# Turning the gathered expert tokens by DMA transposes from SyncE instead of by TensorE

## The chip, the core and the metric

The kernel runs on one core of a Trainium2 chip. A core has a matrix engine (TensorE, PE in the rows; its weight loads are PEld), a vector engine (VectorE, DVE), a scalar engine (ScalarE, ACT), GpSimd (POOL) and SyncE (SP), each with its own instruction stream, and sixteen DMA engines that all issuing engines share. The streams are joined only by semaphores. The metric is the device time of one execution in microseconds. Differences of about 0.2% are what a measurement of this kernel can resolve.

## The reference

Four layers run one after the other on 1250 nodes of 1024 features: a message-passing layer with four hops, a feed-forward layer with low-rank additions, a two-layer neighbour mean network, and last a layer of eight experts. Only the last one is touched:

```python
capacity = max(1, int(Sz * CAP_FACTOR / E) + 1)          # 313 of 1250 tokens
scores = softmax(einsum('bsd,ed->bse', x, router_w))
gate_vals, sel_idx = top_k(swapaxes(scores, 1, 2), capacity)
tokens = x[b_idx, sel_idx]
h = gelu(einsum('becd,edh->bech', tokens, w1) + b1)      # 1024 -> 512
y = einsum('bech,ehd->becd', h, w2) + b2                 # 512 -> 1024
out = zeros_like(x).at[b_idx, sel_idx].add(y * gate_vals)
```

Each expert takes the 313 tokens that score highest for it, so which rows it reads is known only at run time.

## The kernel before, in words

Everything up to the router is the same in both kernels. The experts run from about 1274 us to the end. An expert is e = 2i + j, and j is also its buffer: i counts pairs, j is 0 or 1. `over_experts` (line 197) lays out for every engine a `first`, then a hardware loop over two pairs, then experts 4 to 6 written out, and `last` for expert 7. `after(i, j)` is the next expert.

The normalised tokens lie in DRAM (`h_d`), each row as two float16 parts, high and low, of 1024 elements each. The 313 tokens of an expert fill three lists (`SLOTS`) of 128, 128 and 64 rows. For one expert the engines do this:

- PE makes the lists of token numbers (`lists`, L1476, for the first two experts L1468), DVE turns them into indices (`idx`, L2481), and POOL gathers the rows by three indirect DMAs into `gx` (L857), tokens on the partitions.
- The first product needs the features on the partitions. PE therefore turns `gx` in `turn` (L1484 to L1497): 3 lists x 2 parts x 8 blocks = 48 transposes against an identity into PSUM, and ACT (L1790, high parts) and DVE (L2497, low parts) copy each of the six PSUM banks to `tkT`. `tkT` has two buffers, by j. The turn of expert e+1 stands on PE between `ffn1` and `ffn2` of expert e.
- `ffn1` (L1508): 4 groups h of 24 matmuls of 314 columns, `tkT` times `w1b`. ACT applies the gelu to each group (L1798, to `hb`) and makes its high part (L1802, to `hT`), DVE its low part (L2504, semaphore `s_elo`).
- `ffn2` waits for all four low parts, then runs L1528 (4 x 12 matmuls of 512 columns, with `lists(i + 1, j)` for expert e+2 in its middle) and L1534 (the 64-row list). DVE adds the bias (L2528, L2522), ACT multiplies by the gate (L1809), POOL scatters with addition to DRAM (L865).
- The weights come in float32, 2 MB for each of w1 and w2, by SP's DMA to `w_st` (L1054, one slot for each of the two). ACT makes the high parts (`high`, L1783: to `wb` for w1, to `wa` for w2), DVE the low parts (`low`, L2490). A slot is free for the next load when DVE's low part is made (`s_wlo`).
- SP's stream for expert n is short: `weights(n, 0)`, a wait for the outputs of expert n-2 (`s_y`), the bias rows (L1059, L1061, to a piece of `adj`), `weights(n, 1)`. The very first w1 uses a buffer of its own, so in `sp_first` SP loads w2 of expert 0 and biases and at once goes on to `weights` of expert 1.

`filler` on PE (L1289) multiplies constants and has no result; it stands where PE would be idle.

Of the kernel before, what the change touches and what calls it, by code (L numbers as in the profile page):

```python
# [24 lines left out]
NODES, D = 1250, 1024  # L25
# [192 lines left out]
def build(nc, a):  # L218

    with ExitStack() as ctx:  # L220
# [289 lines left out]
        s_etr, s_eev, s_f1, s_f2, s_gelu, s_ehi, s_elo = (sem("s_" + n) for n in ("etr", "eev", "f1", "f2", "gelu", "ehi", "elo"))  # L510
# [20 lines left out]
        s_gn, s_xg, s_xgl = sem("s_gn"), sem2("s_xg"), sem2("s_xgl")  # L531
        s_tick, s_wsh = sem("s_tick"), sem("s_wsh")
# [88 lines left out]
        def _(g):  # L621
# [229 lines left out]
            def gather(i, j):  # L851
                e = 2 * i + j
                g.wait_ge(s_idx, e + 1)
                g.wait_ge(s_etr, 3 * e + 3)
# [28 lines left out]
        def _(sp):  # L883
# [179 lines left out]

            def sp_first():
                weights(0, 0, 1), biases(0, 0)

            def sp_body(i, j, more):
                n = after(i, j)
                weights(*n, 0)
                sp.wait_ge(s_y, 5 * (2 * i + j) + 2)  # L1070
                biases(*n)
                weights(*n, 1)
# [7 lines left out]
        def _(pe):  # L1080
# [380 lines left out]
            def lists(i, j):  # L1461
# [11 lines left out]
                pe.wait_ge(s_eev, 6 * e + 2)  # L1473
# [7 lines left out]
            def turn(i, j):  # L1481

                e = 2 * i + j
                pe.wait_ge(s_eev, 6 * e + 2)  # L1484
                if isinstance(e, int) and e == 0:
                    pe.wait_ge(s_idx, 2)
                for c in range(3):
                    pe.wait_ge(s_gx[j][c], 16 * (i + 1))
                    if c:
                        pe.wait_ge(s_gelu, 4 * e + 2 * c)  # L1490
                    if c == 2:
                        pe.sem_inc(s_tick, 1)
                    for part in range(2):
                        for k in range(KT):
                            n = SLOTS[c][1]
                            ins = pe.transpose(bank16(2 * c + part)[:, k * P:k * P + n],  # L1496
                                               gx[0:n, j, c, part * D + k * P:part * D + (k + 1) * P], ident16[0:n, 0:n])  # L1497
                    ins.then_inc(s_etr, 1)

            def ffn1(i, j):  # L1500
                e = 2 * i + j
                pe.wait_ge(s_wlo, 2 * e + 1)
                pe.wait_ge(s_eev, 6 * e + 8)
# [35 lines left out]
            def body(i, j, more):  # L1539
                ffn1(i, j), turn(*after(i, j))  # L1540
                ffn2(i, j, (lambda: lists(i + 1, j)) if more else none)

            def first():
# [6 lines left out]
                turn(0, 0)  # L1550
# [5 lines left out]
        def _(s):  # L1556
# [228 lines left out]
            def turn(i, j):  # L1785
                e = 2 * i + j
                for c in range(3):
                    s.wait_ge(s_etr, 3 * e + c + 7)
                    at, n = SLOTS[c]
                    s.activation(tkT[:, j, 0, :, at:at + n],  # L1790
                                 bank16(2 * c).rearrange("p (k n) -> p k n", n=P)[:, :, 0:n], ACT.Copy).then_inc(s_eev, 1)

# [18 lines left out]
            def body(i, j, more):  # L1811
                n = after(i, j)
                high(*n, 0), hidden(i, j), turn(*n), high(*n, 1), gates(i, j)
# [4 lines left out]
            s.sem_inc(s_gelu, 4), s.sem_inc(s_yg, 6), s.sem_inc(s_f1, 8), s.sem_inc(s_f2, 10), s.sem_inc(s_etr, 6)  # L1818
            over_experts(lambda a_, b_, _: s.Fori(a_, b_), lambda: (high(0, 0, 1), turn(0, 0)), body,
# [3 lines left out]
        def _(v):  # L1823
# [668 lines left out]
            def turn(i, j):  # L2492
                e = 2 * i + j
                for c in range(3):
                    v.wait_ge(s_etr, 3 * e + c + 7)
                    at, n = SLOTS[c]
                    v.tensor_copy(tkT[:, j, 1, :, at:at + n],  # L2497
                                  bank16(2 * c + 1).rearrange("p (k n) -> p k n", n=P)[:, :, 0:n]).then_inc(s_eev, 1)

# [31 lines left out]
            def body(i, j, more):  # L2531
                n = after(i, j)
                low(*n, 0), hidden(i, j), turn(*n), keep(i, j)
# [54 lines left out]
```

## Time and profile before

| | us |
|---|---|
| median of three runs | 1536.62 (1533.77 to 1537.14) |
| the profiled execution | 1533.59 |
| its span, first to last instruction | 1532.0 |
| of it, experts from the first turn (1286.39) to the end | 246 |
| TensorE busy | 1463.6 (96%) |
| mean granted TensorE clock | 0.99 |

The profile records one execution. "Idle before" a group is the time its engine did nothing ahead of it, and the arrow names what ended that time. TensorE is busy in nearly all of the span, so a time is read first from its stream, and then from the gaps in it.

### The profile page before, as it was taken

The numbers are of one execution on the slowest core, as the hardware profiler recorded it, in microseconds if no ns is written. First come the engines' busy times: TensorE is split into PE (matmuls) and PEld (weight loads), VectorE is DVE, ScalarE is ACT, GpSimd is POOL, SyncE is SP. The second block draws the span as 40 slices with busy tenths as digits, with TensorE's granted clock in tenths as the row PEclk, the third lists the DMA queues.
The fourth block names the chain that finished last, engine by engine and source line by source line (L and its number), as shares of the span: only waits on it lengthen the run. The fifth ranks groups of instructions, "written<-read, shape, count | busy, mean of one in ns | idle before, by whom it ended". The sixth has DMA issues, their size and how long they took to land.

```text
span 1532.0 us, 30009 instructions
## 1 busy us (share of the span) xinstructions
PE 1463.6 (96%) x9131; PEld 770.0 (50%) x9131; DVE 910.6 (59%) x2039; ACT 588.8 (38%) x803; POOL 384.1 (25%) x399
## 2 busy tenths in 40 slices
PE   6799999999999999999999999999999988999996
PEld 5344454545445545444554454445544545656653
DVE  7888879686978887542342222223336577567542
ACT  4677757373524554221111221001112123655552
POOL 5444320202201110000676000810012211243232
PEclk9999999999999999999999999999999998999998
DMA  6000010000244333221422112531033355888963
GB/s 262 22 22 16 14 42 14 24 3 27 74 151 143 123 132 132 108 82 42 140 80 79 45 41 71 186 113 42 0 107 128 123 197 163 253 235 261 286 170 57
DMA packets 57414, 161.37 MB, mean 105 GB/s; under 512 B 6908, under 2 KB 8395, under 8 KB 57336
## 3 DMA queue, kind: packets, MB, share of 16 engines
q1 hardware_dynamic: 45176, 118.42, 21.4%
q0 software_dynamic: 12160, 41.95, 10.6%
q8 instruction: 44, 0.72, 0.2%
q14 instruction: 34, 0.28, 0.1%
HBM read 118.40 MB, written 41.94 MB: 105 GB/s over the span
## 4 chain that ended last, share of the span: by engine, by line
PE 70%; DVE 14%; issue 7%; ACT 3%; POOL 2%; DVEq 1%; DMA 1%; ACTq 0%; SPq 0%; POOLq 0%
PE ps L1297 27%; PE ps L1369 11%; PE ps L1508 7%; PE ps L1528 5%; PE ps L1188 3%; PE ps L1190 3%; PE ps L1189 3%; PE ps L1116 2%; PE ps L595 2%; DVE bstat L550 1%; PE ps L1534 1%; PE ps L1496 1%; ACT th L1608 1%; DVE hm L1985 1%; PE ps L1217 1%
## 5 line engine op out<-in xcount | busy, mean ns | idle before, releaser
L1297 PE MATMUL ps<-wa,tb 128*128 128x512 f16 x960 | 210.1, 379 | 4.3 <-issue 4.1
L1369 PE MATMUL ps<-adj,nm 128*128 128x384 f16 (+2 forms) x960 | 169.6, 340 | 1.6 <-DVEq L2312 1.6
L1188 PE MATMUL ps<-gp,hop 128*128 (+1 forms) x400 | 151.6, 379 | 0.8 <-DVE gn L2061 0.8
L1189 PE MATMUL ps<-gp,hop 128*128 (+1 forms) x400 | 151.6, 379 | 0.0
L1190 PE MATMUL ps<-gp,hop 128*128 (+1 forms) x400 | 151.6, 379 | 0.0
L1297 PEld LDWEIGHTS ps<-wa,tb 128*128 (+1 forms) x960 | 92.8, 98 | 114.5 <-issue 5.4
L1369 PEld LDWEIGHTS ps<-adj,nm 128*128 x960 | 93.9, 98 | 77.2 <-issue 2.1
L1728 ACT ACTIVATE tb<-cx 128x384 f32 (+1 forms) x48 | 26.8, 559 | 259.1 <-DVE cx L2302 259.1
L1297 PE MATMUL ps<-wa,hop 128*128 128x512 f16 x480 | 105.3, 379 | 2.4 <-DVEq L2240 2.4
L1297 PE MATMUL ps<-wb,hop 128*128 128x512 f16 x480 | 105.1, 379 | 0.0
L1297 PE MATMUL ps<-wb,tb 128*128 128x512 f16 x480 | 103.9, 379 | 0.7 <-DVEq L2326 0.7
L1508 PE MATMUL ps<-tkT,wb 128*128 128x314 f16 x768 | 103.8, 297 | 0.8 <-ACT tkT L1790 0.8
L1508 PEld LDWEIGHTS ps<-tkT,wb 128*128 128x128 f16 x768 | 74.5, 98 | 30.6 <-issue 3.8
L2302 DVE TENSOR_TENSOR cx<-ps,dinv_row 128x384 f32<-128x384 f32 (+1 forms) x48 | 28.9, 602 | 99.2 <-PE ps L1369 99.2
L1528 PE MATMUL ps<-wa,hT 128*128 128x512 f16 x384 | 85.2, 379 | 1.7 <-issue 1.7
L686 POOL DMA_DIRECT2D stage<-in_wn x16 | 9.2, 576 | 279.3 <-PE ps L1297 270.4
L1297 PEld LDWEIGHTS ps<-wb,tb 128*128 (+1 forms) x480 | 46.8, 98 | 57.1 <-issue 0.9
L1990 DVE TENSOR_TENSOR hop<-hm,hop 128x640 f32 (+1 forms) x80 | 68.6, 893 | 11.3 <-ACT hop L1613 11.1
L1297 PEld LDWEIGHTS ps<-wa,hop 128*128 128x128 f16 x480 | 46.2, 98 | 57.6 <-DVEq L2240 2.9
L1297 PEld LDWEIGHTS ps<-wb,hop 128*128 128x128 f16 x480 | 46.4, 98 | 55.3 <-issue 0.4
L692 POOL TENSOR_SCALAR stage<-stage 128x1024 f32<-128x1024 f32 x32 | 34.3, 1073 | 155.0 <-DVE bcur L1927 127.6
L1613 ACT ACTIVATE hop<-hm 128x640 f32 (+1 forms) x80 | 58.9, 736 | 33.6 <-DVE hm L1985 33.5
(403 smaller groups left out, 2459.0 us busy)
## 6 DMA issues: line engine op xcount, KB each, us to landing
w_st<-in_ew SPq DMA_DIRECT2D x16, 2048.0 KB, 11.1
self_d<-cr SPq DMA_DIRECT2D x20, 512.0 KB, 2.9
cr<-self_d SPq DMA_DIRECT2D x20, 512.0 KB, 4.1
stage<-in_wn POOLq DMA_DIRECT2D x16, 512.0 KB, 3.9
x_d<-cr SPq DMA_DIRECT2D x10, 512.0 KB, 3.8
cx<-x_d SPq DMA_DIRECT2D x10, 512.0 KB, 3.6
cr<-x_d SPq DMA_DIRECT2D x10, 512.0 KB, 4.0
out<-cr SPq DMA_DIRECT2D x10, 512.0 KB, 2.7
```

Of the source, the lines that this page charges most:

```text
L595: ins = pe.transpose(bank16(bank + part)[:, k * P:k * P + TP], y_[:, k * P:(k + 1) * P], ident16[0:TP, 0:TP])
L692: link(g.tensor_scalar(st, st, SW ** 0.5, SW ** 0.5, ALU.mult, ALU.mult))
L1116: pe.matmul(ps[:, 2 + j, :], yT[:, j, part, k, :], w1[:, w, k, :], start=(n == 0), stop=(n == 3 * KT - 1))
L1188: pe.matmul(acc, wh, gh, start=(s_ == 0), stop=False, skip_group_check=True)
L1189: pe.matmul(acc, wh, gl, start=False, stop=False, skip_group_check=True)
L1190: return pe.matmul(acc, wl, gh, start=False, stop=(s_ == NT - 1), skip_group_check=True)
L1297: ins = pe.matmul(ps[:, b + c, :], lhs(part, k), w[:, w_, k, c * 512:(c + 1) * 512], start=(k == 0 and part == 0 and w_ == 0), stop=(last ...
L1369: ins = pe.matmul(ps[:, 6 + j, 0:n], nm[:, part, s_, bass.ds(f * P, P)], adj[:, s_, t0 * TP:t0 * TP + n], start=first, stop=(s_ == NT - 1 ...
L1508: ins = pe.matmul(ps[:, 2 + h, 0:FW], w1b[:, j, w_, k * H + h * P:k * H + (h + 1) * P], tkT[:, j, part, k, 0:FW], start=(k == 0 and w_ == ...
L1528: ins = pe.matmul(ps[:, 6 + (j + o) % 2, :], hT[:, part, h, c * P:(c + 1) * P], half(h, w_, o), start=(n == 0), stop=(n == len(terms) - 1))
L1613: s.activation(tile_of(hop[:, h, 0], t).rearrange("p (d n) -> p d n", n=P)[:, :, 0:TP], hm[:, j, :].rearrange("p (d n) -> p d n", n=TP), A ...
L1990: v.tensor_tensor(tile_of(hop[:, h, 1], t).rearrange("p (d n) -> p d n", n=P)[:, :, 0:TP], hm[:, j, :].rearrange("p (d n) -> p d n", n=TP) ...
```

## The change

`turn` is taken out of PE, ACT and DVE, with the semaphores between them (`s_etr`, `s_eev`). SP has a new function, `turn_e(n)`. It waits until `ffn1` of expert n-2 has read the buffer of `tkT`, then for each of the three lists until its gather has landed, and issues two DMA transposes for it, one a part, straight from `gx` to `tkT`: 128 partitions x 1024 elements (64 x 1024 for the last list) to 128 x 8 x 128. Each adds 16 to a semaphore of its own buffer (an older one, `s_xgl`, with its count of 16 taken into account). `ffn1` waits for 96 more of it, and the next gather to that buffer waits for it too.

On SP `turn_e(n)` stands behind `weights(n, 0)` and ahead of the wait for `s_y`, the biases and `weights(n, 1)`; in `sp_first` it stands behind `biases(0, 0)`. DVE's and ACT's other steps keep their order.

```diff
             def gather(i, j):
                 e = 2 * i + j
                 g.wait_ge(s_idx, e + 1)
-                g.wait_ge(s_etr, 3 * e + 3)
+                g.sem_inc(s_tick, 1)
+                g.wait_ge(s_turn[j], TURN_E[j] + 96 * i)
...
+            def turn_e(i, j):
+                e = 2 * i + j
+                sp.wait_ge(s_f1, 4 * e + 4)
+                sp.sem_inc(s_tick, 1)
+                for c, (at, n) in enumerate(SLOTS):
+                    sp.wait_ge(s_gx[j][c], 16 * (i + 1))
+                    sp.sem_inc(s_tick, 1)
+                    for part in range(2):
+                        sp.dma_start_transpose(tkT[:, j, part, :, at:at + n],
+                                               gx[0:n, j, c, part * D:(part + 1) * D]).then_inc(s_turn[j], 16)
+
             def sp_first():
-                weights(0, 0, 1), biases(0, 0)
+                weights(0, 0, 1), biases(0, 0), turn_e(0, 0)
 
             def sp_body(i, j, more):
                 n = after(i, j)
-                weights(*n, 0)
+                weights(*n, 0), turn_e(*n)
...
             def ffn1(i, j):
                 e = 2 * i + j
                 pe.wait_ge(s_wlo, 2 * e + 1)
-                pe.wait_ge(s_eev, 6 * e + 8)
+                pe.wait_ge(s_turn[j], TURN_E[j] + 96 * (i + 1))
...
             def body(i, j, more):
-                ffn1(i, j), turn(*after(i, j))
+                ffn1(i, j)
                 ffn2(i, j, (lambda: lists(i + 1, j)) if more else none)
...
                 filler(16)
-                turn(0, 0)
...
-                high(*n, 0), hidden(i, j), turn(*n), high(*n, 1), gates(i, j)
+                high(*n, 0), hidden(i, j), high(*n, 1), gates(i, j)
...
-                low(*n, 0), hidden(i, j), turn(*n), keep(i, j)
+                low(*n, 0), hidden(i, j), keep(i, j)
```

On PE, in the loop's first body, this is what stands between the last group of `ffn1` and the first of `ffn2` in the kernel before (ISA and REGISTER_ALU are small sequencer steps):

```order
L1508 MATMUL ps<-tkT,wb 128x314 [waits s_gelu]
L1508 MATMUL ps<-tkT,wb 128x314 x23
L1484 ISA
L1488 ISA [waits s_eev]
L1496 MATMUL ps<-ident,gx 128x128 [waits s_gx10]
L1496 MATMUL ps<-ident,gx 128x128 x15
L1490 ISA [waits s_gx11]
L1496 MATMUL ps<-ident,gx 128x128 [waits s_gelu]
L1496 MATMUL ps<-ident,gx 128x128 x15
L1490 REGISTER_ALU [waits s_gx12]
L1496 MATMUL ps<-ident,gx 128x64 [waits s_gelu]
L1496 MATMUL ps<-ident,gx 128x64 x15
```

The same place on PE in the changed kernel, whose line numbers are 7 lower here:

```order
L1501 MATMUL ps<-tkT,wb 128x314 [waits s_gelu]
L1501 MATMUL ps<-tkT,wb 128x314 x23
L1508 REGISTER_ALU
L1509 REGISTER_ALU [waits s_wlo]
L1519 ISA [waits s_elo]
L1521 MATMUL ps<-wa,hT 128x512 [waits s_y]
L1521 MATMUL ps<-wa,hT 128x512 x11
```

The wait for the low parts of the hidden layer, `s_elo`, now follows directly on `ffn1`. On SP, from the loads of expert 0 on, before:

```order
L1054 DMA w_st<-in_ew 128x4x1024 [waits s_h0,s_sc,s_h1,s_N_st1,s_N_st0]
L1059 DMA adj<-in_eb 128x1024
L1061 DMA adj<-in_eb 64x512 x2
L201 UNCONDITIONAL_BRANCH
L201 ISA
L1054 ISA [waits s_wlo]
L1054 DMA w_st<-in_ew 128x8x512
L1070 ISA
L1059 ISA [waits s_y]
```

And on SP in the changed kernel, from the same load on:

```order
L1056 DMA w_st<-in_ew 128x4x1024 [waits s_h0,s_sc,s_h1,s_N_st1,s_N_st0]
L1061 DMA adj<-in_eb 128x1024
L1063 DMA adj<-in_eb 64x512 x2
L1074 DMA_TRANSPOSE tkT<-gx 128x8x128 [waits s_f1,s_gx00]
L1074 DMA_TRANSPOSE tkT<-gx 128x8x128
L1074 DMA_TRANSPOSE tkT<-gx 128x8x128 [waits s_gx01]
L1074 DMA_TRANSPOSE tkT<-gx 128x8x128
L1074 DMA_TRANSPOSE tkT<-gx 128x8x64 [waits s_gx02]
L1074 DMA_TRANSPOSE tkT<-gx 128x8x64
L201 UNCONDITIONAL_BRANCH
L201 ISA
L1056 ISA [waits s_wlo]
```

The load of w1 for expert 1 (128x8x512, the first in the loop) has moved behind the six transposes of expert 0, which wait for gathers.

## Rows read from the trace of the kernel before

**Rows 1.** The page's busy shares (us, share of the span, count).

```profile
PE 1463.6 (96%) x9131; PEld 770.0 (50%) x9131; DVE 910.6 (59%) x2039; ACT 588.8 (38%) x803; POOL 384.1 (25%) x399
```

**Rows 2.** Stretches of the experts: busy us (count) by engine, granted clock, DMA share, GB/s.

```profile
1350.00:1400.00 50.00, 50.00 (x441) 32.54 (x439) 32.92 (x51) 33.37 (x33) 15.01 (x8) 1.00 0.90 273
1400.00:1450.00 50.00, 50.00 (x406) 31.88 (x405) 33.24 (x50) 25.64 (x28) 20.68 (x12) 1.00 0.86 252
```

**Rows 3.** Timeline, expert 6 and the turn of 7: start, us, engine, operation, idle before.

```profile
1465.28 12.97 PE L1508 MATMUL ps<-tkT,wb 128*128 128x314 f16 x96
...
1478.09 2.52 PE L1496 MATMUL ps<-ident,gx 128*128 128x128 f16 x48
1478.29 0.53 ACT L1798 ACTIVATE hb<-ps,eb 128x314 f32<-128x314 f32 x1 [2.18 <-PE ps L1508]
1478.85 0.47 ACT L1802 ACTIVATE hT<-hb 128x314 f16<-128x314 f32 x1
...
1479.35 0.48 DVE L2504 SCALAR_TENSOR_TENSOR hT<-hb,hT 128x314 f16<-128x314 f32 x1 [2.72 <-ACT hT L1802]
...
1480.55 10.53 PE L1528 MATMUL ps<-wa,hT 128*128 128x512 f16 x48
```

**Rows 4.** Timeline, expert 7, which no turn follows.

```profile
1493.72 6.44 PE L1508 MATMUL ps<-tkT,wb 128*128 128x314 f16 x47
...
1506.73 0.52 ACT L1798 ACTIVATE hb<-ps,eb 128x314 f32<-128x314 f32 x1 [2.18 <-PE ps L1508]
...
1507.79 0.49 DVE L2504 SCALAR_TENSOR_TENSOR hT<-hb,hT 128x314 f16<-128x314 f32 x1 [2.71 <-ACT hT L1802]
...
1508.38 10.52 PE L1528 MATMUL ps<-wa,hT 128*128 128x512 f16 x48 [1.68 <-issue]
```

**Rows 5.** Timeline of TensorE, ScalarE and GpSimd around the turn of expert 0.

```profile
1278.87 1.10 POOL L857 DMA_INDIRECT gx<-h_d,idx  x1 [25.57 <-issue]
...
1286.39 2.07 PE L1496 MATMUL ps<-ident,gx 128*128 128x128 f16 x32
...
1288.67 0.62 PE L1496 MATMUL ps<-ident,gx 64*128 64x64 f16 x16 [0.21 <-DMA gx<-h_d,idx]
...
1290.15 12.97 PE L1508 MATMUL ps<-tkT,wb 128*128 128x314 f16 x96 [0.85 <-ACT tkT L1790]
1291.32 3.62 ACT L1783 ACTIVATE wb<-w_st 128x4096 f16<-128x4096 f32 x1
...
1296.32 4.42 DVE L2490 SCALAR_TENSOR_TENSOR wb<-w_st,wb 128x4096 f16<-128x4096 f32 x1
...
1305.41 5.35 PE L1528 MATMUL ps<-wa,hT 128*128 128x512 f16 x24
```

**Rows 6.** SyncE's issues on its timeline: expert 0 and 1's loads, then a steady expert.

```profile
1252.99 0.41 SPq L1054 DMA_DIRECT2D w_st<-in_ew  x1
...
1320.58 0.35 SPq L1059 DMA_DIRECT2D adj<-in_eb  x1
1321.02 1.13 SPq L1061 DMA_DIRECT2D adj<-in_eb  x2
1324.77 4.90 SPq L1054 DMA_DIRECT2D w_st<-in_ew  x2
```

**Rows 7.** DMA issues: KB each and median us to landing; GpSimd's gathers, ns min/median/max.

```profile
w_st<-in_ew SPq DMA_DIRECT2D x16, 2048.0 KB, 11.1
cx<-x_d SPq DMA_DIRECT2D x10, 256.0 KB, 2.7
L857 POOL DMA_INDIRECT gx<-h_d,idx x24: 897/966/1099, 1278.9 to 1461.3; - x24
```

**Rows 8.** Stretches around the filler ahead of expert 0, columns as in rows 2.

```profile
1274.00:1278.00 4.00, 3.30 (x37) 1.65 (x34) 3.16 (x15) 0.00 (x0) 0.00 (x0) 1.00 0.53 154
1278.00:1282.00 4.00, 3.43 (x35) 1.94 (x34) 2.91 (x15) 0.00 (x0) 2.53 (x3) 0.53 0.43 130
1282.00:1286.00 4.00, 4.00 (x13) 1.49 (x12) 0.47 (x4) 0.00 (x0) 3.03 (x4) 0.61 0.92 255
```

**Rows 9.** Timeline of GpSimd and ScalarE in the steady expert 1 (starts 1319.33).

```profile
1315.31 0.91 POOL L857 DMA_INDIRECT gx<-h_d,idx  x1 [0.30 <-issue]
...
1335.65 3.63 ACT L1783 ACTIVATE wa<-w_st 128x4096 f16<-128x4096 f32 x1
```

More of the change, by code:

```diff
@@ L509, in build @@
         s_tok, s_sel0, s_agg = sem("s_tok"), sem("s_sel0"), sem("s_agg")
-        s_etr, s_eev, s_f1, s_f2, s_gelu, s_ehi, s_elo = (sem("s_" + n) for n in ("etr", "eev", "f1", "f2", "gelu", "ehi", "elo"))
+        s_f1, s_f2, s_gelu, s_ehi, s_elo = (sem("s_" + n) for n in ("f1", "f2", "gelu", "ehi", "elo"))
         s_y, s_yg, s_scat, s_scd, s_wld, s_whi, s_wlo, s_b2 = (
@@ L531, in build @@
         s_gn, s_xg, s_xgl = sem("s_gn"), sem2("s_xg"), sem2("s_xgl")
+        s_turn, TURN_E = s_xgl, [16, 16]
         s_tick, s_wsh = sem("s_tick"), sem("s_wsh")
@@ L1472, in lists @@
                 pe.wait_ge(s_sel, e - 1)
-                pe.wait_ge(s_eev, 6 * e + 2)
                 for c in range(3):
@@ L1479, in lists @@
                 ins.then_inc(s_lst, 1)
[L1481 to L1498, printed above, removed]
             def ffn1(i, j):
@@ L1783, in high @@
                 s.activation((w1b, w2b)[m][:, j, 0, :], w_st[:, m, :], ACT.Copy, scale=SW).then_inc(s_whi, 1)
[L1785 to L1791, printed above, removed]
             def hidden(i, j):
@@ L1817, in _ @@
                 s.wait_ge(s_h[j], 16 * (NT // 2))
-            s.sem_inc(s_gelu, 4), s.sem_inc(s_yg, 6), s.sem_inc(s_f1, 8), s.sem_inc(s_f2, 10), s.sem_inc(s_etr, 6)
-            over_experts(lambda a_, b_, _: s.Fori(a_, b_), lambda: (high(0, 0, 1), turn(0, 0)), body,
+            s.sem_inc(s_gelu, 4), s.sem_inc(s_yg, 6), s.sem_inc(s_f1, 8), s.sem_inc(s_f2, 10)
+            over_experts(lambda a_, b_, _: s.Fori(a_, b_), lambda: high(0, 0, 1), body,
                          lambda i, j: (hidden(i, j), gates(i, j)))
@@ L2490, in low @@
                 v.scalar_tensor_tensor(w[:, j, 1, :], w_st[:, m, :], SW, w[:, j, 0, :], ALU.mult, ALU.subtract).then_inc(s_wlo, 1)
[L2492 to L2498, printed above, removed]
             def hidden(i, j):
@@ L2542, in first @@
             def first():
-                places(0, 0), lists(0, 0), places(0, 1), lists(0, 1), turn(0, 0)
+                places(0, 0), lists(0, 0), places(0, 1), lists(0, 1)
                 v.memset(hT[:, :, :, FW:WT], 0.0)
@@ L2550, in last @@
                     out(i, j, c)
-            v.sem_inc(s_eev, 2), v.sem_inc(s_elo, 4), v.sem_inc(s_y, 2), v.sem_inc(s_scd, 2)
+            v.sem_inc(s_elo, 4), v.sem_inc(s_y, 2), v.sem_inc(s_scd, 2)
             over_experts(step.loop, first, body, last, 2 * (4 + 1))
```

## The prediction, as written before the changed kernel was timed

> **What bounds the kernel now.** First read the busy shares: TensorE works in 96% of the span [rows 1]. Then the stretches of the experts: TensorE is busy in 50.00 of 50 us, VectorE in about 33, ScalarE in 26 to 33, and the DMA engines are taken to 0.86 to 0.90 at 252 to 273 GB/s [rows 2]. So TensorE sets the pace of an expert, and the DMA engines stand next in line, not far behind. Last read the timeline of one expert: ffn1 starts at 1465.28, ffn2 at 1480.55, and the turn stands between them with no gap [rows 3]. Expert 7 starts at 1493.72, so an expert takes 28.4 there; from expert 0 at 1290.15 to expert 7 it is 203.57/7 = 29.1 us [rows 4, 5].
>
> **What leaves TensorE, and what it uncovers.** The 48 transposes of a turn fill 2.52 us, 52 ns each [rows 3]. Seven turns stand in the loop, so 7 x 2.45 = 17 us could be hoped for. But look at what ran beside them: the gelu of the last hidden group starts at 1478.29, its high part at 1478.85, its low part from 1479.35 to 1479.83, and ffn2 needs that low part. The turn is the cover of this chain. Expert 7 shows the place without a turn, and there TensorE stands idle for 1.68 us [rows 4]. From the start of ffn1 to that of ffn2 it takes 1508.38 - 1493.72 = 14.66 us; with a turn it takes 1480.55 - 1465.28 = 15.27 us [rows 3, 4]. **A removed turn is worth 0.61 us**, not 2.5. For experts 1 to 6 that is -3.7 us; expert 0 is counted below, expert 7 has none. The six PSUM copies of an expert leave ScalarE and VectorE, which are busy two thirds of the time and are not late at this point: nothing.
>
> **What a DMA transpose costs.** The trace has none. Call G the time that the six of one expert hold SP's queue. Low end: each costs what a plain DMA issue costs on SP, 0.38 us (the two L1061 take 1.13 together, L1054 0.41), six are 2.3 us, and a 256 KB transfer lands 2.7 us after its issue [rows 6, 7]. High end: the queue pays by the row piece. A transposed block is 128 elements of a row, so 320 rows x 2 parts x 8 = 5120 pieces; GpSimd pays 0.966 us for a gather of 128 rows, 7.5 ns a row [rows 7], and 5120 x 7.5 ns = 38.6 us. A middle: SP pays for each of the 40 full 128x128 blocks (2 parts x 2.5 lists x 8) as for one plain issue, 40 x 0.38 = 15 us. The rows nearest to it are SP's own, which say 2.3 to 15; I take **G = 10 us** and keep 2.3 and 38.6 as bounds.
>
> The row says 52 ns for a transpose on TensorE. The Trainium skill (VectorE: DVE Perf Modes, The three transpose paths) lists 390 ns for a 128x128 one on TensorE and 1309 ns by the DMA crossbar, the longest of its three ways. The same skill (Advanced Engine Details and Errata, X-Bar Transpose) says that transposing DMAs are as fast as regular ones, which would leave G near its low end. The two rules disagree, and no row here decides; the first one is a rival below.
>
> **The start.** This is the one turn that nothing can run ahead of. Before, TensorE turned the first two lists at once at 1286.39, waited for the third until 1288.67, and ffn1 started at 1290.15 [rows 5]. The first gather is issued by 1280 and moves 512 KB; at the 255 GB/s of that stretch it has landed by about 1283 [rows 5, 8]. SP then needs 10 us, and the last transpose lands 2.7 us later: ffn1 starts at 1295.7, **+5.5 us**. (G = 2.3: the third list lands at 1288.6, two issues and 2.7 us give 1292, +2. G = 15: +10.6.) TensorE, which was busy with transposes, now stands idle from the filler's end at 1286.4 for 9 us. The trace shows what loosely filled stretches do to its clock: after 3.30 of 4 us busy it was granted 0.53 and 0.61 for eight microseconds, and only then 1.00 again [rows 8]. Eight microseconds at 0.57 lose 3.4 us of work, between the levels 1.2 and 2.4 GHz. I take **+3** for ffn1 of expert 0. It could be nothing, if the clock is kept.
>
> Behind the six transposes on SP stands the load of w1 for expert 1, issued at 1252.99 before [rows 6]. Now it leaves at about 1293 and lands 11.1 us later, at 1304. ScalarE makes its high part ahead of all the gelus of expert 0 (3.6 us, to 1307.7), VectorE its low part (4.4, to 1312.1), and then four low parts of the hidden layer, 4 x 0.48, to 1314. ffn1 ends at 1295.7 + 13.0 + 3 = 1311.7 and its own last chain takes 1.7, to 1313.4. So this load costs **+0.6**. For expert 0 the sum from 1290.15 to ffn2 is 5.5 + 3 + 0.6 - 0.6 (the turn of expert 1 is gone) = +8.5 us.
>
> **The steady experts.** Times are from an expert's ffn1, T = 1319.33. The gathers for expert 2 are issued until 1316.2 [rows 9] and land some 5 us later, T+2. Its transposes hold SP until T+12. Queued behind them are the biases and w2 of expert 2, which left at 1324.77, T+5.4 [rows 6]; now T+12. It lands at T+23, and ScalarE makes the high part to T+27 (before from 1335.65, T+16.3 [rows 9]). VectorE asks for it at the start of the next expert, T+29: 2 us left. w1 of expert 3 goes out right behind, two loads of 2 MB at 250 GB/s need 17 us, so it lands at about T+29 to T+31, and ScalarE wants it at T+30; VectorE can lose 3 us before the last low part is late. So **G = 10 fits, with little to spare: +1 us** over all experts. From G of about 14 the loop from one expert's lists through gather, turn, weights and hidden layer to ffn2 two experts later becomes the longest, and half of each further microsecond falls on every expert (G = 20: +3 each, +18).
>
> **Sum** against the profiled execution (1533.59, span 1532.0): +8.5 - 3.7 + 1 = +5.8 us. The median of the runs is 3.0 us above the profiled one; on the median this gives 1542.4. I write 1542.
>
> **Rivals.**
> (a) *SP's queue becomes the bound.* It decides from the point where G and SP's other 2.3 us of issues (2 x 0.38, 0.35, 1.13) pass the 28.5 us of an expert, G > 26. With G = 38.6 the period is 40.9: 7 x (40.9 - 29.1) = +83, the first turn +34, clock +3: +120, 1657. For it: transposes are cut in pieces, 5120 here, and every expert pays. Against it: a plain issue on SP costs 0.38 us whatever its size. Chance 0.30. By the Trainium skill's 1309 ns (VectorE: DVE Perf Modes, The three transpose paths) 40 blocks would be an estimated 52 us and the time about 1765; this lies in the same rival, and no row tests it.
> (b) *The DMA engines are full.* Share 0.86 x 29.1 = 25 us of packets per expert [rows 2]; 1.31 MB more at 250 GB/s is 5.2, together 30.2 against 28.5. That is +1.7 for seven experts, 12 us more than the forecast: 1554. Against: the share counts packets that wait for each other, and a 2 MB load alone runs faster than in company. Chance 0.17.
> (c) *Cheap transposes.* G = 2.3: start +2, no load late, clock kept, -0.6 and -3.7: 1534 to 1537. Chance 0.09.
> (d) *The hidden chain doesn't show*, and nearly the full turn is saved: 7 x 2.45 = 17 less, +5 at the start: 1524. Expert 7 speaks against it. Chance 0.04.
>
> **How the numbers follow.** The forecast has 0.40 and its own range is 1536 to 1551 (G 4 to 15, clock kept or not). The overall range, 1534 to 1660, takes in (b), (c) and (a) up to G of 39, and leaves out (d), a little of (c), and the part of (a) above it, 0.12: under 0.2 in all. The bound of "same" is 0.2%, what a measurement of this kernel can tell from no change, 1533.5 to 1539.7. Faster is (d) and a trace of (c): 0.05. Same is (c) and a third of the forecast's lower side: 0.21. Slower is the rest: 0.74.
>
> **What would show it.** TensorE idle 1.7 us before L1521 in every expert, with ffn1 to ffn2 at 14.7 us. ffn1 of expert 0 at 1293 to 1301, behind a gap that a transpose ends, and its 96 matmuls longer than 12.97 us. SP's gap between consecutive transposes gives G directly. Wrong if TensorE waits for a transpose in the experts after the first (a), if the loads of w_st take over 14 us (b), or if ffn1 starts with no gap at all.

## The result, and the profile after

The changed kernel takes 1570.38 us (median of four, 1556.64 to 1574.64), beside 1535.19 us for the kernel before on the same chip. The ratio is 1.0216, with a 95% interval of 1.0145 to 1.0287: some 33 to 35 us are lost. The forecast was 1542: the sign and the overall range (1534 to 1660) hold, the forecast's own range (1536 to 1551) and its size do not. The profiled execution after took 1566.17 us, 32.6 more than that of before, and all stretches below come from it. Every ratio in this document is taken over undisturbed executions alone, which leaves out two of the four of the kernel with its loads on ScalarE's queue.

The page of the changed kernel, parts 1 to 3:

```profile
PE 1457.9 (93%) x8747; PEld 754.2 (48%) x8747; DVE 896.9 (57%) x2015; ACT 567.7 (36%) x779; POOL 396.6 (25%) x399
...
DMA packets 99909, 171.83 MB, mean 110 GB/s; under 512 B 49404, under 2 KB 50891, under 8 KB 99832
...
q1 hardware_dynamic: 87672, 128.91, 26.3%
```

and the same two DMA rows of the kernel before:

```profile
DMA packets 57414, 161.37 MB, mean 105 GB/s; under 512 B 6908, under 2 KB 8395, under 8 KB 57336
...
q1 hardware_dynamic: 45176, 118.42, 21.4%
```

TensorE has 384 instructions less and falls from 96% [rows 1] to 93%. The bytes grow by 10.46 MB, eight times the 1.31 MB of an expert's tokens, and the packets under 512 B by 42496, which is 5312 an expert: the 5120 pieces that the prediction counted, and a few. So the transposes do move rows of 128 elements, 256 bytes at a time.

TensorE's timeline after (start, us, engine, line, operation, count, idle before and what ended it):

```profile
1283.43 6.50 PE L1302 MATMUL ps<-ones,ident 128*128 128x512 f16 x16
1302.10 15.05 PE L1501 MATMUL ps<-tkT,wb 128*128 128x314 f16 x96 [12.16 <-DMA tkT<-gx]
1319.03 5.35 PE L1521 MATMUL ps<-wa,hT 128*128 128x512 f16 x24 [1.88 <-DVE hT L2480]
...
1332.95 12.97 PE L1501 MATMUL ps<-tkT,wb 128*128 128x314 f16 x96
1347.73 5.35 PE L1521 MATMUL ps<-wa,hT 128*128 128x512 f16 x24 [1.81 <-DVE hT L2480]
...
1379.06 8.21 PE L1521 MATMUL ps<-wa,hT 128*128 128x512 f16 x24 [4.43 <-DVE hT L2480]
...
1443.86 8.22 PE L1521 MATMUL ps<-wa,hT 128*128 128x512 f16 x24 [6.34 <-issue]
```

The 32.6 us stand in three places:

| stretch | before | after | difference |
|---|---|---|---|
| start to the filler ahead of expert 0 | 1280.87 | 1283.43 | +2.6 |
| filler to ffn2 of expert 0 | 24.5 | 35.6 | +11.1 |
| ffn1 of expert 1 to ffn1 of expert 7 | 174.4 (29.07 each) | 193.2 (32.20 each) | +18.8 |

The first is ahead of anything that the change touches: why the filler starts 2.6 us later in this execution is open. In the second TensorE waits 12.16 us for a transpose, where [rows 5] had 32 of its own at once, and its 96 matmuls take 15.05 instead of 12.97. In the third, the idle time ahead of L1521 reads 1.81, 4.43, 1.81, 6.34, 2.97 and 6.23 us for experts 1 to 6: experts 1 and 3 show what expert 7 showed before [rows 4], experts 2, 4, 5 and 6 are late.

SyncE's timeline after, from the first turn on:

```profile
1285.94 11.71 SPq L1074 DMA_TRANSPOSE tkT<-gx  x6
1298.04 0.42 SPq L1056 DMA_DIRECT2D w_st<-in_ew  x1
1298.81 13.70 SPq L1074 DMA_TRANSPOSE tkT<-gx  x6
...
1315.15 2.29 SPq L1056 DMA_DIRECT2D w_st<-in_ew  x2
1331.47 14.38 SPq L1074 DMA_TRANSPOSE tkT<-gx  x6
...
1347.86 1.46 SPq L1056 DMA_DIRECT2D w_st<-in_ew  x2
...
1425.49 19.32 SPq L1074 DMA_TRANSPOSE tkT<-gx  x6
```

The turns (the six transposes of one expert) that are left out take 15.43 and 14.11, the last two 13.98 and 17.32. Six transposes hold SP for 11.7 to 19.3 us, 15.8 on the mean of experts 2 to 7. The chain that ended last, in order of time, shows how that reaches TensorE, for experts 2 and 3:

```profile
1326.49 4.89 DMA gx<-h_d,idx
1331.47 1.31 SPq L1074
1332.83 3.92 SPq L1074
...
1347.86 0.51 SPq L1056
...
1348.94 18.93 DMA w_st<-in_ew
...
1369.27 3.62 ACT wb L1775
...
1379.06 8.21 PE ps L1521 x24
```

Gather of expert 2, its transposes, then the load of w1 for expert 3, which leaves behind them and lands 18.9 us later (11.1 was the median before [rows 7]); ScalarE makes its high part, and only then the gelus of expert 2, since `high` stands ahead of `hidden` in its stream; ffn2 of expert 2 waits. The stretches after show the resources (columns as in rows 2):

```profile
1350.00:1400.00 50.00, 45.57 (x323) 25.25 (x321) 26.57 (x50) 24.96 (x20) 16.64 (x11) 0.93 1.04 297
1400.00:1450.00 50.00, 41.85 (x281) 24.36 (x279) 25.36 (x39) 18.36 (x22) 16.74 (x8) 0.93 1.15 243
```

Against [rows 2] the DMA share went from 0.90 and 0.86 to 1.04 and 1.15, with no more bytes a second in the second stretch, and TensorE's clock from 1.00 to 0.93.

### The profile page after: what moved, and what is told of

Same layout as the page of the kernel before. It is cut to its first block, busy times and chain, and to the rows that moved or that the text cites. A ratio compares the mean times of both kernels' runs of the same rounds, so it can differ in the third digit from the quotient of the medians.

```text
span 1564.5 us, 29228 instructions
## 1 busy us (share of the span) xinstructions
PE 1457.9 (93%) x8747; PEld 754.2 (48%) x8747; DVE 896.9 (57%) x2015; ACT 567.7 (36%) x779; POOL 396.6 (25%) x399
## 4 chain that ended last, share of the span: by engine, by line
PE 58%; DVE 15%; issue 8%; DMA 7%; SPq 4%; ACT 4%; POOL 2%; DVEq 1%; ACTq 0%; POOLq 0%
PE ps L1310 26%; PE ps L1382 11%; DMA w_st<-in_ew 4%; SPq L1074 3%; PE ps L1201 3%; PE ps L1203 3%; PE ps L1202 3%; PE ps L1521 3%; PE ps L1129 2%; PE ps L596 2%; DMA gx<-h_d,idx 2%; DVE bstat L551 1%; ACT th L1600 1%; ACT wb L1775 1%; DVE hm L1969 1%
## 5 line engine op out<-in xcount | busy, mean ns | idle before, releaser
L1521 PE MATMUL ps<-wa,hT 128*128 128x512 f16 x384 | 94.1, 407 | 27.1 <-issue 17.2
L1501 PEld LDWEIGHTS ps<-tkT,wb 128*128 128x128 f16 x768 | 75.3, 99 | 43.4 <-issue 15.5
L867 POOL DMA_INDIRECT out<-yb,sidx x24 | 64.6, 2690 | 69.9 <-ACT yb L1793 65.9
L1521 PEld LDWEIGHTS ps<-wa,hT 128*128 128x128 f16 x384 | 38.5, 103 | 78.6 <-issue 41.7
L1974 DVE TENSOR_TENSOR hop<-hm,hop 128x640 f32 (+1 forms) x80 | 68.6, 894 | 11.3 <-ACT hop L1605 11.1
```

What stands on the lines that cost most here:

```text
L867: g.indirect_dma_start(out=out_d[:, :] if c < 2 else out_d.rearrange("n (o d) -> (n o) d", o=2), out_offset=bass.IndirectOffsetOnAxis(ap=s ...
L1501: ins = pe.matmul(ps[:, 2 + h, 0:FW], w1b[:, j, w_, k * H + h * P:k * H + (h + 1) * P], tkT[:, j, part, k, 0:FW], start=(k == 0 and w_ == ...
L1521: ins = pe.matmul(ps[:, 6 + (j + o) % 2, :], hT[:, part, h, c * P:(c + 1) * P], half(h, w_, o), start=(n == 0), stop=(n == len(terms) - 1))
L1974: v.tensor_tensor(tile_of(hop[:, h, 1], t).rearrange("p (d n) -> p d n", n=P)[:, :, 0:TP], hm[:, j, :].rearrange("p (d n) -> p d n", n=TP) ...
```

## The experiments

The ratios are always to the kernel before, run on the same chip. Each experiment has a short name here, which the later ones use. The theories were two at first: the transposes' place in SP's queue does the damage (then another order mends it), or their load on the shared DMA engines does.

**Loads first**: all loads ahead of the transposes. From the changed kernel:

```diff
-                weights(0, 0, 1), biases(0, 0), turn_e(0, 0)
+                weights(0, 0, 1), biases(0, 0), weights(0, 1, 0), turn_e(0, 0)
...
-                weights(*n, 0), turn_e(*n)
                 sp.wait_ge(s_y, 5 * (2 * i + j) + 2)
...
                 weights(*n, 1)
+                if more:
+                    weights(*after(*n), 0)
+                turn_e(*n)
```

> The changed kernel, with SyncE's order turned round: for expert n the biases, w2 of n and w1 of n+1 go out first, and the six DMA transposes of n last (at the start w1 of expert 1 goes out ahead of the transposes of expert 0). Bytes and transposes are the same. Theory A (queue order): the experts lost 18.8 us between the first ffn2 and the last because w2 and w1 stood behind about 14 us of transposes on SP; ScalarE's waits for w_st (149 us in sum) all but vanish, TensorE's idle time ahead of ffn2 is 1.8 us in every expert, and the time falls by 15 to 22 us, to 1548 to 1556. Theory B (the DMA engines are full, share 1.0 and more): the order doesn't matter, the loads still land late, and it stays above 1562.

1593.5 us, ratio 1.0385 (1.0366 to 1.0404): worse than the change. Its timeline:

```profile
1363.41 6.18 SPq L1056 DMA_DIRECT2D w_st<-in_ew  x2
1369.80 14.94 PE L1503 MATMUL ps<-tkT,wb 128*128 128x314 f16 x96 [11.98 <-DMA tkT<-gx]
1369.95 18.66 SPq L1074 DMA_TRANSPOSE tkT<-gx  x6
```

The loads are on time now (the idle time ahead of ffn2 is 1.68 to 1.88 us in all experts), and TensorE waits 12 to 14 us ahead of ffn1 in every second expert, for a transpose where the trace names what ended the wait. The transposes begin later and, with loads just issued ahead of them, take 18 to 23 us. Whichever goes first, the other is late: order alone mends nothing.

**Start order**: only the start in another order, w1 of expert 1 ahead of the first turn:

```diff
-                weights(0, 0, 1), biases(0, 0), turn_e(0, 0)
+                weights(0, 0, 1), biases(0, 0), weights(0, 1, 0), turn_e(0, 0)
```

(and `weights` of the expert after at the end of each body, where it was the first step of the next).

> The changed kernel with one thing moved: at the start the load of w1 of expert 1 goes out ahead of the transposes of expert 0; from then on SyncE's order is as in the changed kernel. Theory: ffn1 of expert 0 still waits for the transposes (302 us before, starts about 12 us after the filler), so ffn2 of expert 0 starts no earlier than ffn1's end plus 1.8 us, and the time is within 4 us of the changed kernel, 1565 to 1571. Rival: the late w1 is what cost the start, then it is 8 to 11 us faster than the changed kernel.

1570.55 us, ratio 1.021 (1.0179 to 1.0241), the time of the change. The first ffn1 waits 10.60 in place of 12.16, and its matmuls take 15.77. TensorE is idle for 1.88 us ahead of the first ffn2 in both kernels. So the load of w1 behind the first turn costs nothing that shows; the 0.6 us that the prediction gave it are below what the two medians can tell apart.

**No transposes** at all, `tkT` filled once by GpSimd (the experts' result is wrong for it, and so the kernel shows times alone):

```diff
+            g.wait_ge(s_sc, NT)
+            link(g.memset(tkT[:], 0.5))
...
-                        sp.dma_start_transpose(tkT[:, j, part, :, at:at + n],
-                                               gx[0:n, j, c, part * D:(part + 1) * D]).then_inc(s_turn[j], 16)
+                        sp.sem_inc(s_turn[j], 16)
```

> The changed kernel without its 48 DMA transposes: SyncE waits for the gathers and raises the semaphore itself, and the turned tokens stay at a constant, so the experts' result is left out. Shows what the removed TensorE work is worth when nothing takes its place. Theory (the turn covered the chain of the last gelu): ffn1 to ffn2 takes 14.66 us, TensorE idle 1.7 to 1.8 us ahead of each ffn2, 0.6 us gained per expert and 3 to 4 us at the start, in all 6 to 9 us less than the kernel before, about 1528. Rival (the full turn is worth its time): 2.45 us per expert, 17 to 21 us less than before, 1515.

1548.57 us, ratio 1.0081 (1.0064 to 1.0098), which is 20 us above the expectation, for a reason that has nothing to do with the change (below, under the hardware): the filling holds VectorE up for 8.7 us, the filler starts 11 us later, and ffn2 of expert 0 waits 12.87 us for the hidden layer, which stands behind a load that left later in turn. The steady experts are what it was made for, and they are clear:

```profile
1355.33 5.35 PE L1522 MATMUL ps<-wa,hT 128*128 128x512 f16 x24 [1.81 <-DVE hT L2481]
1384.10 5.35 PE L1522 MATMUL ps<-wa,hT 128*128 128x512 f16 x24 [1.88 <-DVE hT L2481]
```

From ffn1 of expert 1 (1340.54) to that of 7 (1511.68) an expert takes 28.52 us, beside 29.07 before. So **the removed turn is worth 0.55 us**, not 2.5, and nothing is late when the transposes are away.

**Expert 0 on TensorE**, turned as before, and the later experts by DMA; this is the kernel "start order" with the old transposes, PSUM copies and their semaphores for expert 0:

```diff
-                weights(0, 0, 1), biases(0, 0), weights(0, 1, 0), turn_e(0, 0)
+                weights(0, 0, 1), biases(0, 0), weights(0, 1, 0)
+                sp.wait_ge(s_eev, 6)
+                sp.sem_inc(s_turn[0], 96)
```

> As e2_start_order, and expert 0 is turned by TensorE and the six PSUM copies as in the kernel before; experts 1 to 7 by the DMA transposes as in the changed kernel. Theory: the start costs 11 us of the 32 lost, so the time is 9 to 12 us under e2_start_order, about 1557, and ffn1 of expert 0 starts within 4 us of the end of the filler. Rival: the lost time at the start only moves to expert 1, whose transposes now stand late as well, and the gain is under 4 us.

1551.51 us, ratio 1.0112 (1.0093 to 1.0131): 19 us less than "start order", more than expected. ffn1 of expert 0 starts at 1290.75 and ffn2 at 1305.60, against 1300.64 and 1318.29 there, which is 12.7; the rest comes in the later experts, whose code is the same in both, and no run shows why. This kernel is the base of the next ones. Its first turn by DMA, at 1291.11 in a quiet stretch, takes 8.94 us. The later ones take 14.03, 14.83, 13.65, 16.96, 17.42, 16.18, and an expert takes 31.6 us. What stretches them? Two kinds of traffic run beside them: the weight loads, and GpSimd's scatters with addition.

**Light weights**: the loads from w2 of expert 1 on are cut to 32 KB each, and the experts compute with old values in the rest.

```diff
+                else:
+                    sp.dma_start(w_st[:, m, 0:64], v[:, 0, 0:64]).then_inc(s_wld[m], 16)
```

> e4_start_on_tensor with the loads of the experts' weights, from w2 of expert 1 on, cut from 2 MB to 32 KB each (the rest of the staging buffer keeps old values, so the experts after the first are computed with wrong weights). Order, transposes, gathers, scatters and the computing engines' work are unchanged. Theory C (the transposes are slow because they share the sixteen DMA engines with 4 MB of weights an expert): SyncE is held 9 to 10 us by six transposes, as in the quiet stretch of e4 (8.94), not 14 to 17, no wait for w_st is left, and the time is 1528 to 1533. Theory D (the transposes have their own price of 14 us or more on SyncE): it is held 14 us again, and only the waits for weights go.

1544.57 us, ratio 1.0076 (1.0046 to 1.0106). Neither theory had this: the turns alternate, 9.09, 22.53, 8.49, 22.23, 8.48, 23.22, 8.50. Two of them with GpSimd's issues around them:

```profile
1348.46 8.49 SPq L1078 DMA_TRANSPOSE tkT<-gx  x6
1353.05 3.56 POOL L868 DMA_INDIRECT out<-yb,sidx  x1 [6.62 <-ACT yb L1810]
...
1377.96 1.61 POOL L868 DMA_INDIRECT out<-yb,sidx  x1 [0.30 <-issue]
1378.62 22.23 SPq L1078 DMA_TRANSPOSE tkT<-gx  x6
1380.16 1.58 POOL L868 DMA_INDIRECT out<-yb,sidx  x1 [0.60 <-issue]
1382.91 4.21 POOL L868 DMA_INDIRECT out<-yb,sidx  x1 [1.16 <-ACT yb L1810]
```

Where the first scatter is issued 4.6 us after the turn has begun, 8.5 us; where the scatters run through it, 22. That points to the scatters, which the next two take away. Why it is 22 us here, and 14 to 17 with full loads, no run shows.

**No scatters**, with light weights and with the full ones, on the kernels "light weights" and "expert 0 on TensorE" (the experts' sums never reach the output):

```diff
-                    g.indirect_dma_start(out=out_d[:, :] if c < 2 else out_d.rearrange("n (o d) -> (n o) d", o=2),
-                                         out_offset=bass.IndirectOffsetOnAxis(ap=sidx[:, j, c:c + 1], axis=0),
-                                         in_=yb[:, c, :] if c < 2 else yb[:, c, 0:512], in_offset=None,
-                                         compute_op=ALU.add).then_inc(s_scat, 16)
+                    g.sem_inc(s_scat, 16)
```

> e7_light_weights without the experts' scatters (POOL raises the semaphore instead; the experts' sums are left out, and the weights are stale as in e7). What is left on the DMA engines of an expert is the gather, the biases and the transposes. Theory E (a queue of 256-byte pieces gets a small share of an engine while another queue sends 4 KB packets on it; in e7 six transposes took 8.5 us when no scatter ran and 22 to 23 us when one did): SyncE is held 8.5 to 10 us in every expert, and an expert takes 28.6 us. Rival F (SyncE is slow in every second expert for a reason of its own, buffer or address): the 22 us come back in every second expert.

> e4_start_on_tensor with full weight loads and without the experts' scatters (their sums are left out). Theory E: since weights and transposes are in the same queue one behind the other, only gathers meet the transposes; SyncE is held 9 to 11 us (14 to 17 in e4), the loads of w_st leave 5 us earlier, an expert takes 28.6 to 29.5 us (31.6 in e4) and the time is 1525 to 1533, of which about 2 us are the last scatter that is missing at the end. Rival: the weight loads themselves hold the transposes up, and it stays above 1540.

With light weights 1522.05 us in a single execution, turns of 8.42 to 9.65. With full weights 1525.96 us, ratio 0.9939 (0.9922 to 0.9955), and:

```profile
1322.55 8.04 SPq L1072 DMA_TRANSPOSE tkT<-gx  x6
...
1350.71 8.19 SPq L1072 DMA_TRANSPOSE tkT<-gx  x6
```

All seven turns take 8.0 to 9.5, a w_st load lands after 10.0 (median), and an expert takes 28.52 us, the time of a kernel with no transposes at all. Scatters without transposes cost nothing either (the kernel "no transposes" kept them, at 28.52).

The kernels with and without scatters (full weights, expert 0 on TensorE) differ in the scatters alone, but one thing changes with them. Without scatters the loads have landed before each turn begins (issued at 1304.9, the longest landing 12.0, turn at 1322.6). With scatters they are later, and in five of the six slow turns weight packets still run in the first 3 to 6 us. What separates scatters from loads is the one slow turn with no weight packets in it, the 14.03 us at 1319.14. These are the DMA queues (packets, MB, share of 16 engines; q1 has SyncE's DMAs, q0 GpSimd's) over that turn:

```profile
q1 hardware_dynamic: 4497, 1.12, 57.9%
q0 software_dynamic: 487, 1.47, 56.3%
```

and over the turn at 1322.55 of the kernel with no scatters:

```profile
q1 hardware_dynamic: 4774, 1.18, 78.0%
q0 software_dynamic: 35, 0.10, 3.4%
```

Q1's packets are some 250 bytes each in both, so they are the transposes' pieces and no weights: with scatters the turn takes 14.03, without them 8.04. The changed kernel has two such turns, 14.38 (at 1331.47) and 14.11 (at 1396.90). So **the scatters alone bring a turn from about 8 to about 14 us**, and no other traffic is needed for it. Loads in flight do it too: in "loads first" the turn at 1297.47, with 4 MB just issued and no scatter near, takes 21.65 us, and the one at 1298.81 of the changed kernel, with one w1 ahead, 13.70. The longest turns of the changed kernel, 17.32 and 19.32, have both.

**Loads on ScalarE's queue.** If the order of SP's queue is what hurts, another queue for the loads should free them. On the kernel "expert 0 on TensorE":

```diff
-                weights(*n, 1)
-                if more:
-                    weights(*after(*n), 0)
...
+                    if more is not None and h == 2:
+                        load(*after(i, j), 1)
+                    if more and h == 3:
+                        load(*after(*after(i, j)), 0)
```

> e4_start_on_tensor with the weight loads of w2 of n and w1 of n+1 issued by ScalarE's DMA queue, between its gelus of expert n-1 (after the second and the third), as soon as their slot is free; SyncE keeps only transposes and biases. Theory A (queue order on SyncE: loads stood behind transposes): w_st lands in time, TensorE's idle time ahead of ffn2 falls to 1.8 us in each expert, and the time is 1530 to 1537. Theory B (the DMA engines are full, whoever issues): transposes and loads slow each other, SyncE is held about 20 us as in e1, and it stays within 5 us of e4, 1547 to 1556.

1562.84 and 1576.31 us, ratio 1.0222 (1.0169 to 1.0274), above both theories (1530 to 1537 and 1547 to 1556). Its trace is not read here. The next kernel adds one thing, the lists of expert e+2 ahead of ffn2 and ahead of VectorE's `out`, so that gathers leave sooner:

```diff
-                ffn2(i, j, (lambda: lists(i + 1, j)) if more else none)
+                if more:
+                    lists(i + 1, j)
+                ffn2(i, j)
```

> e8_weights_on_act, and TensorE makes the lists of expert e+2 between ffn1 and ffn2 of expert e, where it is otherwise idle for the last gelu, not in the middle of ffn2; VectorE turns them into indices ahead of its first output of the expert, so the gathers start about 5 us earlier. Theory: the lists' 0.75 us go into the idle time, 0.7 us less in each of six experts than e8, 4 us in all, and the transposes start earlier; 1526 to 1533. Rival: the gathers then meet the weight loads on the DMA engines and it is no faster than e8.

1578.75 us, ratio 1.0297 (1.026 to 1.0333), where 1526 to 1533 had been expected. Its timeline:

```profile
1343.53 44.71 SPq L1075 DMA_TRANSPOSE tkT<-gx  x6
...
1418.34 40.84 SPq L1075 DMA_TRANSPOSE tkT<-gx  x6
```

With the loads in a queue of their own the transposes are not behind them but beside them, and take 18 to 45 us after the first turn of 9.02; TensorE waits 4.53 and 10.28 us for them, and up to 20.66 us ahead of an ffn1 where the trace names no releaser. The queue order was mended and the time got worse: that speaks for the shared engines and against the order of SP's queue.

**Early lists** alone, on the kernel "expert 0 on TensorE", with the loads on SyncE:

> e4_start_on_tensor, and the lists of expert e+2 made between ffn1 and ffn2 of expert e, so that gathers start 5 to 6 us earlier (weights on SyncE as in e4). Theory: the transposes start some 5 us earlier, still meet gathers and scatters, and w2 leaves 3 to 5 us earlier; 1541 to 1548. Rival: earlier gathers only meet the weight loads, and it is within 3 us of e4.

1550.14 us, ratio 1.0109 (1.0092 to 1.0125) beside 1.0112: nothing that counts, as the rival had it. The lists' matmuls do go into the gap (1.08 to 1.15 us are left of it where nothing is late), and the turns start earlier, but still meet the scatters, and now more of the loads: 15.5 to 19.8 us.

**Scatters that wait for the transposes**, to keep the two apart, on the kernel "early lists":

```diff
                     gather(i + 1, j)
+                    g.wait_ge(s_turn[j], TURN_E[j] + 96 * (i + 2))
+                    g.sem_inc(s_tick, 1)
                 scatter(i, j)
```

> e12_early_lists with one wait added: GpSimd issues the scatter of expert e only when the transposes of expert e+2 have landed. Bytes and instructions are the same. Theory E: the transposes run alone in 9 to 10 us, w2 leaves on time and the time is 5 us or more under e12, 1533 to 1541, though the scatter comes some 8 us later. Rival G (the sixteen engines are full whatever the order): the scatter's bytes only move onto the weight loads, and it is as slow as e12 or slower.

The turns: 8.67, 11.82, 9.23, 9.08, 8.92, 9.00, 8.79. The separation works; the one of 11.82 still meets a load. The time is 1573.69 us, ratio 1.0263 (1.0246 to 1.028), where 1533 to 1541 had been expected. The price has moved:

```profile
1346.73 7.86 PE L1528 MATMUL ps<-wa,hT 128*128 128x512 f16 x24 [10.16 <-DVE yb L2528]
...
1415.57 7.58 PE L1528 MATMUL ps<-wa,hT 128*128 128x512 f16 x24 [6.67 <-DVE yb L2528]
```

The late scatter keeps `yb`, VectorE can't write the next outputs into it, PSUM is not emptied, and TensorE stands in the middle of ffn2.

**One list of three by DMA.** Last a smaller dose, on the kernel before: from expert 1 on list 0 by two DMA transposes, lists 1 and 2 by TensorE in the gap of the gelu chain:

```diff
+                for part in range(2):
+                    sp.dma_start_transpose(tkT[:, j, part, :, 0:P],
+                                           gx[:, j, 0, part * D:(part + 1) * D]).then_inc(s_turn[j], 16)
...
-                weights(*n, 0)
+                weights(*n, 0), turn_e(*n)
...
+                    if c == 0 and not full:
+                        pe.sem_inc(s_etr, 1)
+                        continue
```

> The kernel before, with a third of the change: from expert 1 on only the first list of 128 tokens is turned by two DMA transposes on SP's queue (behind that expert's w1 and b2, ahead of the scatter wait and the next loads); lists 1 and 2 are turned by TensorE and two PSUM copies each, as before, and in banks that are free by then (32 transposes, about 1.5 us, beside the gelu chain). Expert 0 is turned wholly by TensorE, so the start of the experts is that of before. Theory (the gain is the uncovered turn, the cost is SP's hold beside GpSimd's scatter-adds, so the dose decides): 2 of 6 transposes carry 2/5 of the bytes, 3.2 to 3.8 us alone by the 8.0 to 9.5 us of six, 6 to 8 us beside scatters; the loads behind them leave that much later, which the idle before w2's need covers in most experts. The row ahead of ffn2 stays near 1.7 us, an expert takes 28.5 to 28.9 us in place of 29.07, and the whole is 1 to 4 us shorter than the kernel before (ratio 0.997 to 0.9995). Rival: the DMA engines are full already (share 0.86 to 0.90 before), so that any further pieces come out in the weight loads' landing: an expert takes 29.3 us or more, some experts show 2 us and more idle ahead of ffn2, and the whole is 2 us or more longer than before (ratio over 1.001).

1540.99 us (median of 11), ratio 1.0039 (1.0027 to 1.0052): a little slower, as the rival had it, though the profiled execution is one that went by the theory. It took 1530.34, the fastest of the eleven (the next is 1535.21), and it shows the fit:

```profile
1386.72 2.70 PE L1530 MATMUL ps<-tkT,wb 128*128 128x314 f16 x19
1389.25 1.63 PE L1517 MATMUL ps<-ident,gx 128*128 128x128 f16 x32
1391.22 5.35 PE L1550 MATMUL ps<-wa,hT 128*128 128x512 f16 x24 [0.34 <-DVE hT L2532]
```

32 transposes fill the gap, SP's two take 2.9 to 5.9 us a turn, six experts take 28.73 us each (1317.73 to 1490.11), and the rows ahead of ffn2 are 0.2 to 0.4 but for one of 1.65. The ten other executions lie 5 to 14 us above it, 1535 to 1545, where the kernel before spreads over 1532 to 1538 in sixteen. What they lost isn't in a trace, so that full DMA engines are the reason there is argued and not shown. What can be said: in one execution of eleven two fifths of the bytes fit, on DMA engines that its trace shows at 1.02 to 1.06, and in the others the time was lost again.

## Why the prediction came out as it did, step by step

1570 lies inside the overall range more by its width than by the reasoning. The range reaches up to rival (a), SP's queue as the bound with a G of up to 39 us, and that did not happen. By the prediction's own rules a G of 20 (+15.5 at the start, +18 in the experts) gives about 1570, but G was 11.7 at the start and 15.8 on the mean of experts 2 to 7, and with these the same rules give about 1549. The parts one by one:

**The removed turn is worth 0.61 us an expert.** Right: 0.55 by the kernel without transposes. Whoever had counted the 2.5 us of [rows 3] would have been out by 12 us over the experts.

**G = 10 us.** Right for six transposes alone (8.0 to 9.5, 128x1024 elements in 1.27 us on the median of 42), and wrong where they are used: 13.7 to 19.3 beside the scatters and loads of the changed kernel. The step that failed is this term: G was taken as one number, the work of one queue, between bounds from SP's issue cost and from GpSimd's rows, and what else is in flight had no part in it. The DMA share of 0.86 to 0.90 [rows 2] stood only in rival (b), as bytes: 5.2 us of them. The transposes fill the engines for longer than that: the 8.04 us of the turn alone at 78.0% are 6.3 us of all sixteen, the 14.03 us of the one beside scatters at 57.9% are 8.1. In the changed kernel the share of 1.04 and 1.15 goes with 297 and 243 GB/s, beside 273 and 252 before. Rival (b) came nearest, with about half of the price (12 us for the experts, 22 measured) and no word of the scatters; rival (a) had its price at the wrong place: G never came near 26 in the changed kernel.

Six transposes are 40 blocks of 128x128, so in 8.5 us a block takes 0.21 us of the queue. The Trainium skill (VectorE: DVE Perf Modes, The three transpose paths) gives 1309 ns for one; worked out from that, an estimated 52 us for six, which no run here comes near except where two queues run into each other (44.71). The other sentence of the Trainium skill, that transposing DMAs are as fast as regular ones (Advanced Engine Details and Errata, X-Bar Transpose), is the nearer one, but not met: 1.31 MB in 8.5 us is 154 GB/s, and a 2 MB load landed in 10.0 us, 210 GB/s.

**The start, +5.5, +3 for the clock, +0.6 for w1.** The sum to ffn2 of expert 0 was +8.5 and measured +11.1. ffn1 started 12 us later by the clock of the trace, of which 2.6 had come from ahead (the first gather leaves at 1281.42, not at 1278.87); what is left is 9.4 beside the forecast 5.5. The transposes began about when the forecast, moved by those 2.6 us, puts them (1285.94), but held SP for 11.71 us and not for 10, while the gathers of experts 0 and 1 still ran beside them, and ffn1 started 4.5 us after SP was free again, not 2.7. The clock term holds: 96 matmuls in 15.05 instead of 12.97, +2.1 of the 3, with a granted clock of 0.50 and 0.64 in the two stretches of 6 us around 1302. The +0.6 for w1 is not seen (1.88 us of idle time ahead of ffn2 with w1 behind the turn and ahead of it). That the start is a dear place the kernel "expert 0 on TensorE" shows: 12.7 us of its gain are there, with one turn of eight.

**The steady experts, +1.** This is where the miss lies, 22 us of it. Against the 28.52 each of the kernel without transposes, six experts took 193.2 - 171.1 = 22.1 us more. 13.1 of it is idle ahead of ffn2 beyond the usual 1.68 to 1.81 (2.62 + 4.66 + 1.29 + 4.55), and 9.0 is the clock after it: the first 24 matmuls of L1521 take 8.21, 8.22 and 7.03 instead of 5.35, and expert 6's 48 take 12.07 instead of 10.52. The loop that the prediction named, lists, gather, turn, weights, hidden layer, is the one in the chain above. Its time table can be laid beside it (T = 1332.95, ffn1 of expert 1). The transposes are done at T+12 by the forecast and at T+12.9 measured. They took 14.4, but had begun 3.5 us sooner than forecast. The loads of w2 and w1 leave at T+12 to T+13 by the forecast and from T+14.9 measured; the bias rows stand ahead of them with 1.8 us, which the forecast left out. They have landed at T+29 to T+31 by the forecast and at T+35 measured, since 4 MB took 20 us and not 17, on engines that the next transposes share. The need was at T+30. So the slack of w1 was none even by the forecast's own table, and only +1 us was put on it. Nor does its rule for a longer G carry the miss: from about 14 half of each further microsecond falls on every expert, which for 15.8 is 0.9 us each, some 5 in all, beside 22. Whether 14 was the right threshold these rows don't say: the turn of 15.43 is followed by an expert that is not late, the one of 14.11 by one with 6.34 us of idle time. The clock was counted at the start, by [rows 8], and left out here, where 0.50 to 0.66 stand behind the waits of experts 2 and 4 (last section) and the slower matmuls cost two thirds as much again as the idle time.

**What was named as signs.** "TensorE idle 1.7 us before L1521 with ffn1 to ffn2 at 14.7" holds in two of the six experts 1 to 6 (1.81). "Wrong if TensorE waits for a transpose after the first" did not happen: it waits for w1's load, through ScalarE. "Wrong if loads of w_st take over 14 us" did: 18.9 in the chain above, 21.8 for the longest.

## What to carry to other kernels

Price a DMA that is added not by its own duration and not by its bytes alone, but by what is in flight on the same sixteen engines at that minute, here scatters with addition above all. The mean share of the DMA engines does not tell whether there is room: without scatters it stands at 0.92 to 0.94 and nothing is late, and from 0.86 to 0.90 before the change the transposes did not fit beside the scatters. Ask what the removed work was covering: here four fifths of the hoped-for gain (1.9 of 2.45 us an expert) was not there to be had. And where an engine is made to wait a few microseconds for a late load, add the slower clock after the wait to the wait itself.

## What the runs showed of the hardware

- A DMA transpose of 128x1024 two-byte elements holds SyncE's queue for 1.2 to 1.3 us when nothing else is in flight, and up to 6.0 us beside scatters and loads (1217/2264/6033 ns over the 48 of the changed kernel, 1207/1271/2178 over the 42 without scatters). Six hold it 8.0 to 9.5 us alone and 14.0 to 14.4 beside scatters with no load in flight; with the light weights it was 22 to 23 beside scatters. Why the scatters do this, by their read and write back, their rows or their queue's turn at the engines, no run here separates.
- With the weight loads in a second queue beside them, six take 18 to 45 us: worse, not better.
- After a wait of 4.4 or 6.3 us in the midst of full work TensorE does its next 24 matmuls of 512 columns in 8.2 us in place of 5.35, after one of 2.97 us in 7.03, and after one of 1.8 us in 5.35. The stretches around the wait of expert 2 show the clock (columns as in rows 2); the level of 2.4 GHz is left for that of 1.2 in the second, and is back in the fourth:

```profile
1374.00:1378.00 4.00, 0.63 (x5) 0.23 (x3) 4.00 (x3) 3.81 (x9) 0.00 (x0) 1.00 1.11 209
1378.00:1382.00 4.00, 2.94 (x7) 1.04 (x8) 1.19 (x6) 0.00 (x0) 0.00 (x0) 0.51 1.13 255
1382.00:1386.00 4.00, 4.00 (x13) 1.55 (x12) 0.69 (x1) 0.00 (x0) 0.00 (x0) 0.64 0.97 299
1386.00:1390.00 4.00, 4.00 (x46) 2.22 (x45) 1.43 (x6) 0.00 (x0) 0.04 (x1) 1.00 1.00 396
```

- In the kernel without transposes a fill of `tkT` on GpSimd held up VectorE for just as long as it lasted. The two engines' timelines:

```profile
1255.26 8.63 POOL L883 MEMSET tkT<- 128x10240 f16 x1 [0.33 <-POOL tokg L847]
```

```profile
1255.23 8.71 DVE L2431 TENSOR_SCALAR bits<-bits 128x56 int32<-128x56 int32 x1
```

An operation of 56 elements that takes 0.19 us elsewhere took 8.71. An experiment's own filling can cost more than what it is to measure; it has to go where nobody is in a hurry.
